# Rows of the sorted token buffer: 320 floats in place of 273

## The reference

```python
logits = x @ gate_weight.T                      # x = xn, 64 experts
topk_w, topk_idx = top_k(softmax(logits), 8)    # 8 experts a token, weights made to sum to 1
expanded = repeat(x, 8); order = argsort(flat_ids)
sorted_tokens = expanded[order]                 # 8192 rows, sorted by expert
g = ragged_dot(sorted_tokens, w_gate, group_sizes)
u = ragged_dot(sorted_tokens, w_up, group_sizes)
out = ragged_dot(silu(g) * u, w_down, group_sizes)
y = sum(out[inv] * topk_w)
```

## Time and profile before

| what | value |
|---|---|
| time, median of 3 runs | 475.41 us (472.82 to 475.66) |
| span of the profiled execution | 549.4 us |
| instructions in the profile | 9474 |
| expert stage, first to last add of results in the profile | 346.05 to 529.69 us |
| tiles of the expert stage | 90 |
| one load of rows | 136.5 KB, 128 pieces of 1092 bytes |

### The profile page before, as it was taken

One profiled execution on the slowest core, in us unless ns is written; L12 is line 12 of the kernel. 1 busy time (PEld: TensorE's weight loads), 2 busy tenths in 40 slices (PEclk: granted clock), 3 DMA queues, 4 the chain that ended last, 5 costly groups with the idle time before them and its releaser, 6 DMA issues.

```text
span 549.4 us, 9474 instructions
## 1 busy us (share of the span) xinstructions
PE 380.1 (69%) x2230; PEld 254.9 (46%) x2234; DVE 273.4 (50%) x1082; ACT 170.4 (31%) x413; POOL 221.1 (40%) x188
## 2 busy tenths in 40 slices
PE   4667776491212029999999998788888879888820
PEld 1325353250100015554553636676776768677710
DVE  5454789241001017788680404455656556556515
ACT  1122100140100015465466672333333333333310
POOL 3540000067777700000000000677777777777740
PEclk9978855567555559999999999999999998999875
DMA  6878999953233300700000027899999999999998
GB/s 187 156 210 209 197 170 183 319 201 107 108 113 112 113 20 2 154 2 2 1 2 1 2 83 240 210 288 267 276 275 292 283 285 256 275 283 285 269 237 260
DMA packets 91051, 95.24 MB, mean 173 GB/s; under 512 B 8979, under 2 KB 83091, under 8 KB 91027
## 3 DMA queue, kind: packets, MB, share of 16 engines
q1 hardware_dynamic: 64851, 65.42, 44.7%
q0 software_dynamic: 16032, 20.75, 18.7%
q10 hardware_dynamic: 10144, 8.79, 5.0%
HBM read 56.61 MB, written 31.89 MB: 161 GB/s over the span
## 4 chain that ended last, share of the span: by engine, by line
PE 26%; DMA 16%; issue 16%; SPq 11%; another core or an unknown queue 11%; POOL 9%; DVE 7%; ACT 2%; POOLq 1%; DVEq 0%; ACTq 0%
POOL y_acc L603 9%; PE ps L827 8%; DMA y_acc<-att_raw,dst 7%; PE ps L849 7%; SPq L388 6%; PE ps L808 5%; DMA qk_parts<-part_lo 3%; SPq L412 2%; DMA probs<-y_acc 2%; DMA qz<-neg_lo 2%; DVE mx_low L1134 2%; PE ps L830 2%; ACT probs L660 1%; DVE ps L1131 1%
## 5 line engine op out<-in xcount | busy, mean ns | idle before, releaser
L603 POOL DMA_INDIRECT y_acc<-att_raw,dst x90 | 139.8, 1553 | 197.8 <-ACT att_raw L706 166.9
L660 ACT ACTIVATE probs<-ps 128x128 f32<-128x128 f32 (+3 forms) x192 | 85.5, 491 | 177.9 <-PE ps L830 100.9
L827 PE MATMUL ps<-qz,kz 128*128 128x128 f32 (+3 forms) x192 | 76.1, 447 | 55.9 <-issue 27.4
L940 PE MATMUL ps<-att,probs 128*96 128x128 f32 x720 | 96.1, 277 | 3.6 <-issue 2.7
L592 POOL DMA_INDIRECT slots<-rows,slot_i x64 | 61.8, 966 | 89.2 <-DVE rows L1069 70.0
L808 PE MATMUL ps<-kz,qz 96*128 96x512 f32 (+3 forms) x192 | 75.9, 470 | 31.1 <-DVE mx_low L1134 18.0
L940 PEld LDWEIGHTS ps<-att,probs 128*96 128x96 f32 x720 | 89.5, 166 | 14.1 <-issue 6.6
L1131 DVE CUSTOM_DVE_ANT_0 ps<-ps,mask_qk 128x512 f32<-128x512 f32 (+3 forms) x128 | 61.2, 504 | 52.8 <-remote 41.6
L827 PEld LDWEIGHTS ps<-qz,kz 128*128 128x128 f32 x192 | 39.8, 212 | 90.1 <-issue 43.8
L947 PE MATMUL ps<-probs,hidden_sb 96*128 96x256 f32 x180 | 60.1, 416 | 29.2 <-DVE hidden_sb L1221 22.1
L1134 DVE TENSOR_REDUCE mx_low<-ps 128x1 f32<-128x512 f32 x64 | 44.1, 689 | 58.0 <-PE ps L808 29.5
(11 more groups left out here) (137 smaller groups left out, 291.2 us busy)
## 6 DMA issues: line engine op xcount, KB each, us to landing
probs<-w_gu SPq DMA_DIRECT2D x96, 192.0 KB
v_aug<-slots SPq DMA_DIRECT2D x96, 136.5 KB
probs<-w_down ACTq DMA_DIRECT2D x88, 96.0 KB
y_acc<-zero SPq DMA_DIRECT2D x12, 384.0 KB
qz<-qk_parts SPq DMA_DIRECT2D x16, 256.0 KB, 7.4
qz<-zero SPq DMA_DIRECT2D x3, 1024.0 KB
probs<-y_acc SPq DMA_DIRECT2D x3, 1024.0 KB, 10.1
qk_parts<-part_hi SPq DMA_DIRECT2D x8, 256.0 KB, 4.0
```

Source lines behind the costliest of these rows:

```text
L603: pool.indirect_dma_start(y_acc[u][:, :], bass.IndirectOffsetOnAxis(ap=dst[u][:, 0:1], axis=0), y_sb[u], None, compute_op=ALU.add).then_in ...
L660: act.activation(probs[:, step % 2, j, lo:hi], ps[:, B_BANKS[n % len(B_BANKS)], lo % HALF:(hi - 1) % HALF + 1], ACT.Exp, scale=DK ** -0.5) ...
L827: last = pe.matmul(bank[:, a:b], head_rows(kz, g, j, kt, P), qz[g % SLOTS][:, lo // HALF, j, a:b], start=True, stop=True, skip_group_check ...
L940: last = pe.matmul(ps[0:I, 2 + b, w * P:(w + 1) * P], wgu[u][:, (2 * c + w) * I:(2 * c + w + 1) * I], xgT[b][:, c * P:(c + 1) * P], start= ...
```

## The change

ROW becomes 320. A row of `slots` and of `rows` is then 1280 bytes in place of 1092; the 47 floats behind the weights carry nothing. GpSimd sets those and the ones up to the row's end to zero once, early on, and waits for that before its first scatter. Everything that is computed from ROW follows by itself: the size of the scatters and of the loads of rows, the place of `xg` in `v_aug` (it starts at float 1536 of 4096 in place of 1912), the width of the DMA that zeroes the spare rows, and the address of each SBUF buffer that is allocated after `rows` (1504 bytes further up in each partition). `done` stays 5: ceil(2184 / 512) and ceil(2560 / 512).

```diff
-ROW = D + 1 + 2 * K
+ROW = 320
@@ GpSimd, after ones and minus_half
             link(pool.memset(minus_half[:, :], -0.5))
+            pool.memset(rows[:, :, WGT + K:ROW], 0.0).then_inc(s_zero, 1)
             for lo, hi in zip(LN_BATCHES, LN_BATCHES[1:]):
@@ GpSimd, ahead of the scatters
             pool.wait_ge(s_route, 1)
+            pool.wait_ge(s_zero, 3)
             pool.wait_ge(s_sloti, 1)
```

## The result

The changed kernel takes 473.79 us (median of 18 runs, 468.23 to 478.50) against 475.64 us for the kernel before in the same comparison (18 runs). The ratio is 0.9936, with a 95% interval of 0.9909 to 0.9963: about 3 us faster. (Runs in a slower state, 4 of the changed kernel's 18, are left out of all ratios, which so are no quotients of the medians; and three profiles of such runs, the first of the changed kernel and those of even_not_256 and all_256_xg, are left out of the means of the expert stage.) I had forecast 2 us slower. The time lies in my range (471 to 483), but the sign is the other one. Run again later, the change gave 0.9944 (0.9905 to 0.9984).

What follows compares the result with a forecast made beforehand. POOL sets the expert stage's floor, nearly level with the landing of adds. Slower row loads delay landings, +2.0 us; scatters, memset, spare rows and moved buffers nothing: 475.41 to 477.4 us, range 471 to 483.

Steps and rivals of the forecast that it cites:

- item 5: Zeroing of spare rows on SP: under 0.1 us; buffers behind rows move by 1504 bytes a partition: taken as nothing.
- the very rule of the Trainium skill: DRAM reads of rows start at the 256-byte boundary below: 38.5 beats before, 40 after, so no gain from padding.
- Step 1: Loads of rows from slots: about 64 ns a piece, 5 to 7 more than 58.8; 69 means no gain from alignment.
- Rival B: Loads of rows: whole multiples are much cheaper to read; -4 us, 471.4 us; chance 0.06.
- Step 2: Expert stage: +2.0 us; POOL's shortest interval still 1.86 us, mean 2.07 to 2.10, landings on the chain near 5.9.
- rival A: Expert stage: DMA engines are its clock, so all DMA time counts, +3.3 to +4.9 us; 480.8 us; chance 0.19.
- Steps 3 and 4: Scatters still 0.96 us each, ended before 195 us; new memset on POOL done before 4.98 us, about 0.4 us, hidden.
- the cover: Between scatters and first reader of slots or overwriting of rows: more than 110 us, hiding dearer scatters.
- Rival C: Stall at the scatters comes from uneven writes; profile would lose up to 60 us, timed run 469.4 us; chance 0.07.

Runs made afterwards that it cites:

- even_not_256: Kernel before with unused tiles putting all large buffers on multiples of 64 bytes but not of 256; 0.9978 of before.
- all_256_xg: Kernel before, rows of 273, every large SBUF buffer on multiples of 256 bytes, plus xg buffers 1280 bytes apart instead of 1092; 0.9753 of before.
- layout_only: Kernel before, ROW 273, with an unused 1504-byte tile behind rows, so later buffers lie where the change puts them; 0.9875 of before.
- layout_undone: Changed kernel, ROW 320, with 32 unused bytes behind rows, restoring later buffers' places to multiples of 64 and 256; 1.0021 of before.
- before_look: Kernel before, unchanged, profiled again beside the variants; 552.68 us, on a chip with the stall at the scatters.
- load_273: Changed kernel, but each load of rows takes only the first 273 of 320 floats, 1092 bytes from even places; 0.9886 of before.
- zero_256: Kernel before with only zero, the source of all clearing DMAs, moved onto a multiple of 256 bytes; 0.9919 of before.
- staging_256: Kernel before with only v_aug, qz0, qz1, kz0 and kz1 moved onto multiples of 256 bytes; 0.9992 of before.
- layout_only_again: layout_only run once more, as base for change_again in the same call; 0.9958 of before, 472.17 us.
- change_again: The changed kernel as it is, run again in the same call as layout_only_again; 0.9944 of before, 472.35 us.
- row_320_all_even: Changed kernel with 96 unused bytes ahead of the buffers of the front, so all large buffers are even; 0.9888 of before.

## Why the prediction was wrong

**The step that failed** is item 5, its last sentence: the buffers behind `rows` move by 1504 bytes, "no row prices that, and I take nothing". For a gain by it I had left a chance of 0.02. It was the one part with an effect larger than my sum. layout_only alone gives -5.9 us in one run and -2.0 in the other; layout_undone takes the gain away. Eight profiles tell where. Attention begins at 105.3 to 107.8 us in the three with the buffers' places of before (before, before_look, layout_undone), and at 101.5 to 102.9 in the five with the change's (both of layout_only, both of the change, load_273): 2 to 6 us sooner, 4.1 in the mean. A single profile can't say how much of it reaches the end: from there to the first add it takes 162.1 us in layout_undone, and 165.4 and 162.1 in the two of the changed kernel. The medians say that. The chain of waits ahead of it runs through the SP queue and the DMAs of clearing and staging (the issue of the clearings alone is 29.1% of the chain of 0 to 110 us in before_look, 27.2% in the changed kernel and 18.1% in all_256), and the 512-byte pieces of the first clearing are 8% quicker there (48.1 to 44.4 ns), because their source came to lie 128 and no longer 160 bytes beyond a multiple of 256. That the place of `zero` alone has an effect on the time is shown (zero_256, 0.9919). But there it saved 13 ns a piece, and the change saves 3.7: in proportion, an estimate, 0.23% or about 1 us of the 2 to 6 us. So the source explains only a part of the gain. That the targets take part is likely from the rates, not shown in a time: staging_256 moved only them and gained nothing that can be seen (0.9992). The moved buffers are shown as the cause; how the gain divides among them is open.

I had cited the very rule of the Trainium skill that is named above, and applied it to the DRAM side of one transfer only. On that side the runs don't bear it out in the time: even rows of 1092 bytes took 62.9 and 63.1 ns in the two kernels that have them, uneven ones 62.3 on average, where the rule gives 35 beats against 38.5, an estimate. It shows strongly in the clearing, and weakly in the stores of `part_hi`.

**Step 1, the cost of a piece**: the difference right, the level not, and the reason wrong. 1280 bytes were to take 5 to 7 ns more; they take 6.4 (62.4 to 68.8). But a piece was to take about 64 ns, and 69 was my mark for no gain from alignment; that mark is met, and load_273 shows the same. My base of 58.8 ns was from 1 us of the trace, 3.6 too low, and that the difference came out is partly luck. Rival B (a gain from whole multiples) is refuted by load_273 and by these pieces.

**Step 2, what of it becomes time**: +2.0 us, measured as +1.0 (layout_undone, 1.9 either way), and for the pair layout_only_again and change_again as -0.7 by the ratios and +0.2 by the medians (2.5 either way). None of these is clear of nothing. POOL's shortest interval stayed at 1.85 us, as the step had it. The landings on the chain were to be near 5.9 us; the changed kernel has eleven of 6.3 us on average, but layout_only, with the rows of before, has eleven of 6.2, so the rows didn't make them. Two of the changed kernel's, in the chain of waits:

```profile
267.53 6.30 DMA y_acc<-att_raw,dst
...
349.92 7.31 DMA y_acc<-att_raw,dst
```

The stage itself speaks for a larger cost. With loads of 1280 bytes it lasts 184.5 to 188.1 us in four profiles (mean 186.1), with 1092 bytes 179.7 to 185.2 in thirteen (mean 182.3). The difference is 3.9 us, 1.8 either way, nearer to rival A (+3.3 to +4.9) than to my +2.0. Where the rest of it goes in the medians isn't settled. PE still waits for no load, so one mark of A, loads that come late, is absent; its other, a mean interval over 2.12 us, is just reached (2.12 and 2.11 us in the two profiles of the changed kernel). A is neither shown nor refuted.

**Steps 3 and 4**: right. The last scatter starts at 189.4 us in the changed kernel, 38 us ahead of the first overwriting of `rows` (227.5) and 51 us ahead of the first load of rows; the cover is smaller than the more than 110 us that I read, since those had the stall in them, and still ample. The memset took 0.41 us within POOL's idleness. POOL at the start, in time, the changed kernel:

```profile
2.44 0.41 POOL L546 MEMSET rows<- 128x376 f32 x1
4.75 0.73 POOL L549 TENSOR_TENSOR rstd<-var_eps,minus_half 128x2 f32<-128x2 f32 x1 [1.90 <-DVE var_eps L987]
```

**Rival C**, uneven writes as the cause of the stall: refuted. row_320_all_even has rows of 1280 bytes and takes 548.55 us on the chip with the stall. What holds the engines on such a chip stays open.

## A version that beats both

all_256: ROW stays 273, and every large SBUF buffer is allocated on a multiple of 256 bytes. 0.9772 and 0.9769 of before in two runs, one on either kind of chip: 463.07 us where the kernel before took 474.54. Nothing else in the kernel is touched. In its two profiles attention begins at 94.98 and 96.69 us, 9 to 13 us sooner than in the two of the kernel before (105.30 and 107.75). Tensor engine in time, all_256:

```profile
94.98 0.47 PE L828 MATMUL ps<-qz,kz 128*128 128x128 f32 x1 [2.11 <-DMA qz<-neg_lo]
```

So the gain of 11 us lies in the front, where DMAs from SBUF to SBUF and to DRAM move pieces of 512 bytes. The expert stage, which my expectation had as perhaps shorter, is not: 181.1 and 185.2 us. The wait for `qz<-neg_lo`, 6.69 us before, is down to 2.11.

## What to carry to other kernels

A change of a tile's size moves everything that is allocated behind it. Before the size is judged, place an unused tile of the same number of bytes there and time that; and undo the move under the change. Where DMAs read the same short piece of SBUF again and again, as in a clearing, allocate it on a multiple of 256 bytes; with the other large buffers aligned too, all_256 gained more than `zero` alone did, but what each buffer gives isn't shown. And compare a profile's span with the median only when both are of one chip.

## What the runs showed of the hardware

In the first clearing, from SBUF to SBUF with one source for all pieces, a DMA packet of 512 bytes takes 34 to 35 ns when its source begins on a multiple of 256 bytes, 44 ns at 128 beyond, 48 to 49 at 160 and 52 at 192; the target, at 0, 32 or 64, changes that by 1 to 2 ns. Stores of 512-byte pieces from SBUF to DRAM take 26 to 29 ns, with 2 ns between a source at 0 and at 192. A load of 1092 bytes from DRAM takes 62 ns on even and on uneven places alike. And there are chips (or states of one) on which every engine but POOL all but stands still for some 75 us while 64 scatters are issued, with the scatters' packets at 31% of the DMA engines, and chips on which nothing of the sort happens: 475 and 552 us for one and the same kernel.
